# Projecting g by channels in two column tiles and turning it with four transposes, in an attention kernel on one core

## What is computed

```python
g     = (einsum('bchw,oc->bhwo', x, w_g) + b_g).reshape(B, N, Ci)
theta = (einsum('bchw,oc->bhwo', x, w_theta) + b_theta).reshape(B, N, Ci)
phi   = (einsum('bchw,oc->bohw', x, w_phi) + b_phi[:, None, None]).reshape(B, Ci, N)
att   = softmax(einsum('bnc,bcm->bnm', theta, phi), axis=-1)
y     = einsum('bnm,bmc->bnc', att, g).reshape(B, H, W, Ci)
out   = einsum('bhwc,oc->bohw', y, w_out) + b_out[:, None, None]
inv   = bn_gamma / sqrt(bn_var + 1e-5)
return x + out * inv[:, None, None] + (bn_beta - bn_mean * inv)[:, None, None]
```

## Time and profile before

| | |
|---|---|
| Runs | 204.07, 204.53, 207.46 us; median 204.53 us |
| Profiled execution | 204.88 us, its span 203.1 us |
| Mean granted clock of TensorE | 0.998 |
| PE busy | 193.6 us (95%) |
| PE weight loads busy | 133.3 us (66%) |
| DVE busy | 175.2 us (86%) |
| ACT busy | 136.2 us (67%) |
| POOL busy | 152.3 us (75%) |
| DMA moved | 35.28 MB, most packets under 512 B |

### The profile page before, as it was taken

The page is one execution under the profiler, slowest core; times in us unless marked ns, Lnnn a source line. Parts: engine busy times, 40 slices in busy tenths (PEclk is TensorE's granted clock), DMA queues, the critical chain, the costliest instruction groups (busy, mean ns, idle before and its releaser), DMA issues.

```text
span 203.1 us, 3988 instructions
## 1 busy us (share of the span) xinstructions
PE 193.6 (95%) x1100; PEld 133.3 (66%) x1100; DVE 175.2 (86%) x291; ACT 136.2 (67%) x245; POOL 152.3 (75%) x127
## 2 busy tenths in 40 slices
PE   7997889999999999999999999999999998999993
PEld 6575756686666857677666957677566956566551
DVE  0689898978997899978998899978998899989881
ACT  2866867768396856866587766866577675767731
POOL 2458898699779999699988999699988964954300
PEclk9999999999999999999999999999999999999999
DMA  6315998899999999899779997899998998847102
GB/s 156 97 34 163 225 114 174 185 221 175 186 227 232 217 163 231 184 257 207 187 163 253 229 215 168 161 246 189 195 214 181 223 170 181 138 76 155 52 3 103
DMA packets 59500, 35.28 MB, mean 174 GB/s; under 512 B 50400, under 2 KB 50912, under 8 KB 59488
## 3 DMA queue, kind: packets, MB, share of 16 engines
q1 hardware_dynamic: 59200, 35.01, 83.0%
q10 hardware_dynamic: 288, 0.14, 0.3%
HBM read 8.36 MB, written 4.23 MB: 62 GB/s over the span
## 4 chain that ended last, share of the span: by engine, by line
PE 70%; DVE 12%; DMA 5%; issue 4%; ACT 3%; SPq 1%; POOL 1%; ACTq 0%; POOLq 0%; DVEq 0%
PE ps_scores L743 22%; PE ps_flip L808 12%; PE ps_y L755 12%; PE ps_misc L769 6%; PE ps_y L762 6%; DVE neg_max L599 6%; PE ps_misc L727 5%; PE ps_misc L849 4%; DMA pt_hi<-p_hi 3%; DVE pt_lo L637 3%; DMA vec<-vectors_dram 2%; SPq L292 1%; DVE y_norm L616 1%; PE ps_scores L755 1%; ACT probs L532 1%
## 5 line engine op out<-in xcount | busy, mean ns | idle before, releaser
L532 ACT ACTIVATE probs<-ps_scores,neg_max 128x1024 f32<-128x1024 f32 x64 | 71.9, 1123 | 30.0 <-DVE neg_max L599 15.1
L599 DVE TENSOR_REDUCE neg_max<-ps_scores 128x1 f32<-128x1024 f32 x64 | 77.9, 1218 | 9.1 <-PE ps_scores L743 8.8
L637 DVE SCALAR_TENSOR_TENSOR pt_lo<-ps_flip,pt_hi 128x512 f16<-128x512 f32 x84 | 53.9, 684 | 5.4 <-ACT pt_hi L519 5.1
L519 ACT ACTIVATE pt_hi<-ps_flip 128x512 f16<-128x512 f32 x84 | 45.6, 595 | 14.2 <-PE ps_flip L808 14.2
L426 POOL TENSOR_TENSOR p_lo<-probs,p_hi 128x1024 f16<-128x1024 f32 x22 | 47.0, 2138 | 4.3 <-POOL p_hi L422 3.4
L743 PE MATMUL ps_scores<-phi_hh,theta_hl 128*128 128x512 f32 x128 | 47.1, 449 | 3.1 <-ACT probs L532 2.5
L808 PE MATMUL ps_flip<-ident,probs 128*128 128x128 f32 x336 | 44.5, 275 | 0.7 <-DVE pt_lo L637 0.7
L808 PEld LDWEIGHTS ps_flip<-ident,probs 128*128 128x128 f32 x336 | 38.1, 142 | 9.6 <-DVE pt_lo L637 2.5
L743 PE MATMUL ps_scores<-phi_ll,theta_hl 128*128 128x512 f32 x128 | 40.1, 394 | 0.0
L755 PE MATMUL ps_y<-pt_hi,g_parts 128*128 128x512 f16 x120 | 28.4, 379 | 0.5 <-issue 0.4
L422 POOL TENSOR_SCALAR p_hi<-probs 128x1024 f16<-128x1024 f32 x22 | 23.5, 1067 | 6.7 <-ACT probs L532 6.3
(11 more groups left out here) (79 smaller groups left out, 175.3 us busy)
## 6 DMA issues: line engine op xcount, KB each, us to landing
x_in<-x_in_dram SPq DMA_DIRECT2D x16, 256.0 KB, 3.3
inv_all<-inv_row SPq DMA_DIRECT2D x15, 256.0 KB, 4.0
out_dram<-resid SPq DMA_DIRECT2D x15, 256.0 KB, 2.8
phi_hh<-hi SPq DMA_DIRECT2D x14, 256.0 KB, 5.8
phi_ll<-lo SPq DMA_DIRECT2D x14, 256.0 KB, 6.1
theta_hl<-hi SPq DMA_DIRECT2D x7, 256.0 KB, 4.7
theta_hl<-lo SPq DMA_DIRECT2D x7, 256.0 KB, 5.6
pt_hi<-p_hi SPq DMA_TRANSPOSE x22, 4.0
```

The source lines that it names most:

```text
L519: nc.scalar.activation(pt_hi[ring][:, c * HALF_TILES:(c + 1) * HALF_TILES, slot * P:(slot + 1) * P], ps_flip[c][:, :].rearrange("p (a n) - ...
L532: nc.scalar.activation(probs[k % PROB_RING][:, :], ps_scores[k % 2][:, :], ACT.Exp, bias=neg_max[:, k % STEPS:k % STEPS + 1], accum_out=ro ...
L599: nc.vector.tensor_reduce(out=top, in_=ps_scores[k % 2][:, :], op=ALU.max, axis=AX.X, negate=True).then_inc(row_max_ready if by_dma(it, k) ...
L637: nc.vector.scalar_tensor_tensor(out=pt_lo[ring][where], in0=ps_flip[c][:, :].rearrange("p (a n) -> p a n", n=P), scalar=PROB_SCALE, in1=p ...
```

## The change

In image b at j = 4 nothing is projected any more. At j = 5, behind the low-half sum, PE projects g with the operands exchanged: `wg` (64 columns) is the stationary and 512 positions of `x_in` move, once into partitions 0 to 63 and once into 64 to 127 of `ps_misc`. The bank then holds channels on partitions and positions along the row. ACT evacuates this at j = 6 into the new tile `g_channels`; DVE takes the peak from there. At j = 7, where PE has no flips, it turns `g_channels` with four transposes into the second flip bank, ACT evacuates that bank into `g_raw` at its j = 7, and the flips at the next j = 0 wait for it before they write that bank. The convolution at j = 6 waits for the evacuation into `g_channels`, and POOL's split waits for the evacuated theta and phi instead of the projection of g.

```diff
--- before.py
+++ after.py
@@ -104,6 +104,7 @@
         phi_hh = [sbuf(f"phi_hh{i}", [P, N], F32R) for i in range(2)]
         phi_ll = [sbuf(f"phi_ll{i}", [P, N], F32R) for i in range(2)]
         g_raw = [sbuf(f"g_raw{i}", [P, MT, CI], F32) for i in range(2)]
+        g_channels = sbuf("g_channels", [P, BANK], F32)
         g_scaled = sbuf("g_scaled", [P, MT, CI], F32)
         g_parts = [sbuf(f"g_parts{i}", [P, MT, 2 * CI], F16) for i in range(2)]
         g_peak = sbuf("g_peak", [P, 2], F32)
@@ -165,6 +166,8 @@
         lo_ready = sem("lo_ready")
         g_ready = sem("g_ready")
         g_out = sem("g_out")
+        g_channels_out = sem("g_channels_out")
+        g_flipped = sem("g_flipped")
         g_peak_ready = sem("g_peak_ready")
         g_peak_spread = sem("g_peak_spread")
         g_peak_read = sem("g_peak_read")
@@ -440,7 +443,7 @@
                                             g_parts[r][:, :, 0:CI], ALU.subtract).then_inc(g_split, 1)
 
                 if j == 5 and exists(b + 2, B):
-                    hold(g_ready, b + 2)
+                    hold(proj_out, 2 * b + 2)
                     split_x(it * 16 + 16 * (k // STEPS + 2), r, 0)
                     split_x(b + 2, r, 1)
                 if j == 7 and exists(b + 2, B):
@@ -543,9 +546,15 @@
                     nc.scalar.activation(qk[:, c * BANK:(c + 1) * BANK], ps_misc[:, :], ACT.Identity,
                                          bias=BIAS_TP).then_inc(proj_out, 1)
 
-                if j == 5 and exists(image + 1, B):
+                if j == 6 and exists(image + 1, B):
                     act.wait_ge(g_ready, image + 2)
-                    evacuate_g(image + 1, ps_misc[:, :], g_raw[(k // MT + 1) % 2][:, :, :].rearrange("p t c -> p (t c)"))
+                    wait(act, g_peak_ready, image + 1)
+                    wait(act, g_flipped, image)
+                    nc.scalar.activation(g_channels[:, :], ps_misc[:, :], ACT.Copy).then_inc(g_channels_out, 1)
+                if j == 7 and exists(image + 1, B):
+                    act.wait_ge(g_flipped, image + 1)
+                    evacuate_g(image + 1, ps_flip[1][:, :].rearrange("p (a c i) -> p a c i", c=PER_IMAGE, i=CI),
+                               g_raw[(k // MT + 1) % 2][:, :, :].rearrange("p (c a) i -> p a c i", c=PER_IMAGE))
 
                 if j == 0:
                     exponential(it, k)
@@ -583,10 +592,15 @@
                                                op0=ALU.add, op1=ALU.subtract).then_inc(first_lo, 1)
 
             def peak_of_g(b, r):
-                dve.wait_ge(g_out, b + 1)
                 wait(dve, g_peak_spread, b - 1)
-                nc.vector.tensor_reduce(out=g_peak[:, r:r + 1], in_=g_raw[r][:, :, :], op=ALU.max, axis=AX.XY,
-                                        apply_absolute_value=True).then_inc(g_peak_ready, 1)
+                if is_first(b):
+                    dve.wait_ge(g_out, 1)
+                    nc.vector.tensor_reduce(out=g_peak[:, r:r + 1], in_=g_raw[r][:, :, :], op=ALU.max, axis=AX.XY,
+                                            apply_absolute_value=True).then_inc(g_peak_ready, 1)
+                else:
+                    dve.wait_ge(g_channels_out, b)
+                    nc.vector.tensor_reduce(out=g_peak[:, r:r + 1], in_=g_channels[:, :], op=ALU.max, axis=AX.X,
+                                            apply_absolute_value=True).then_inc(g_peak_ready, 1)
 
             def read_peak(b, r, spread):
                 dve.wait_ge(g_peak_spread, b + 1)
@@ -803,6 +817,8 @@
                         if isinstance(f, int) and f == 0:
                             pe.wait_ge(*((g_out, 1), (shift_ready, 1))[c])
                         wait(pe, pt_lo_ready, 2 * f + c - 1)
+                        if j == 0 and c == 1 and not in_last_half(t):
+                            wait(pe, g_out, image + 1)
                         for a in range(HALF_TILES):
                             m = c * HALF_TILES + a
                             last = nc.tensor.transpose(ps_flip[c][:, a * P:(a + 1) * P],
@@ -822,6 +838,14 @@
                     pe.wait_ge(g_split, image_at(it, k - 6) + 1)
                     wait(pe, y_scaled, h)
                     sum_high(ring, r, ps_y, slice(0, BANK), slice(0, BANK))
+
+                if j == 7 and exists(image + 1, B):
+                    pe.wait_ge(g_channels_out, image + 1)
+                    pe.wait_ge(pt_lo_ready, 2 * flip_at(it, k - 3) + 2)
+                    for a in range(HALF_TILES):
+                        last = nc.tensor.transpose(ps_flip[1][:, a * P:(a + 1) * P],
+                                                   g_channels[:, a * P:(a + 1) * P], ident[:, :])
+                    last.then_inc(g_flipped, 1)
 
                 t = tile_at(it, k + 1)
                 if exists(t, TILES):
@@ -852,15 +876,19 @@
                 h = half_at(it, k - 10)
                 if j % HALF_TILES == 2 and exists(h, HALVES - 2):
                     if more:
-                        pe.wait_ge(*((proj_out, 2 * image + 2) if j == 2 else (g_out, image + 2)))
+                        pe.wait_ge(*((proj_out, 2 * image + 2) if j == 2 else (g_channels_out, image + 1)))
                     else:
                         wait(pe, result_ready, h)
                     convolve(h, ps_misc[:, :], slice(0, BANK))
 
-                if j == 4 and more:
+                if j == 5 and more:
                     pe.wait_ge(proj_out, 2 * image + 2)
                     wait(pe, result_ready, 2 * image - 1)
-                    project_g(ps_misc, (k // MT + 1) % 2, range(MT)).then_inc(g_ready, 1)
+                    for c in range(PER_IMAGE):
+                        last = nc.tensor.matmul(ps_misc[c * CI:(c + 1) * CI, :], wg[:, :],
+                                                x_in[(k // MT + 1) % 2][:, c * BANK:(c + 1) * BANK],
+                                                start=True, stop=True, skip_group_check=True)
+                    last.then_inc(g_ready, 1)
 
 
                 if tile_is(it, k, 1):
```

## The result

The changed kernel takes 208.0 us (median of its runs) where the kernel before took 204.3 beside it: a ratio of 1.0137, 95% interval 1.0093 to 1.0182. It is slower, by less than 2%. The forecast was 207.4, a ratio of 1.014. The profiled execution took 208.06 us with a span of 206.2, 3.1 more than the earlier trace rows.

A forecast was written before the change was run, and what follows sets the result against it. The prediction took PE as the bound, its work laid nearly end to end; terms summed to +0.43 us an image, taken as +2.9 over seven images, giving 207.4 us from 204.53. Its range was 204.0 to 210.6.

The forecast's parts named there:

- Step 2: Tile 3's flips, now right behind tile 5's scores, wait for DVE's low part of tile 2: about +0.62 us an image.
- Step 3: Two column-tiled projections at j = 5 behind the low-half sum, overlapping only partly: +1.29 us an image, bounds 0.86 and 1.72.
- Step 1: The eight projections at j = 4 leave PE's chain: -1.73 us an image.
- step 4: Four PE transposes of g_channels added at j = 7: +0.44 us an image, bounds 0.4 and 0.6.
- the second rival: The two projections at j = 5 run wholly side by side, 0.86 us; image unchanged, 204.5 us; chance 0.16.
- Step 5: The convolution at j = 6 no longer waits for DVE's y_norm: -0.19 us an image, bounds -0.19 and 0.
- Step 6: One more ACT evacuation, and tile 7's exponential waiting at j = 7, stay hidden: 0 us, bounds 0 and +0.3.
- Step 7: DVE's peak, waiting for ACT's evacuation at j = 6, and POOL's x split with its changed hold: both 0.
- side by side: no change: Rival at j = 5: both projections overlap wholly, 0.86 us, image changes by 0.00; 204.5 us, chance 0.16.
- One after the other: Rival at j = 5: the column tiles run in single file, 1.72 instead of 1.29 us; 210.5 us, chance 0.25.
- The wait of step 2 does not show: Rival at tile 3's flips: no wait; 203.2 us with partial overlap (chance 0.05), 200.2 with whole overlap (0.04).

The follow-up runs named there:

- e6: Changed kernel with SP's DMA transpose of tile 1's high part issued ahead of the three low-part restacks; 205.7 us, ratio 1.0027.
- e1: Changed kernel with the two column-tiled projections back at j = 4 and their ACT evacuation at j = 5; 206.1 us, ratio 1.0034.
- e2p: Kernel before with its eight old projections moved to j = 5 and DVE's 128x2 scaling written as two 128x1 instructions; 209.2 us, ratio 1.0212.
- e4p: Changed kernel with g_raw's evacuation behind tile 7's exponential and DVE's 128x2 scaling written as two 128x1 instructions; 206.7 us, ratio 1.0057.
- e2: Kernel before with its eight old projections moved from j = 4 to j = 5, evacuation to j = 6; 218.85 us, ratio 1.0664.
- e4: Changed kernel with ACT's evacuation into g_raw moved behind tile 7's exponential; 213.9 us, ratio 1.0453.
- e3: Changed kernel with the pair of projections at full width, w_g padded with zero columns, accumulating one after the other; 212.8 us, ratio 1.0352.
- e8: Changed kernel with the pair at j = 4, tile 1's transpose ahead of low restacks, and 128x2 scaling as two 128x1; 203.2 us, ratio 0.9862.
- e10: Kernel before, old projections kept at j = 4, with tile 1's transpose ahead of low restacks and 128x2 scaling as two 128x1; 204.5 us, ratio 0.9976.
- e6b: Kernel before with SP's transpose of tile 1's high part issued ahead of the low-part restacks; 204.6 us, ratio 0.999.

## Why the prediction was right, and where it was not

The time was right, and by luck in good part: two terms were wrong, and the errors and the waits that had no term made up for each other. With steps 2 and 3 as measured the prediction's own sum is -1.73 + 0.83 + 0.86 + 0.44 - 0.19 = +0.21 an image, which would have given about 206 us. That is near what e6 takes, where PE no longer waits for tile 1's transfer: 205.7.

1. *Step 1* (-1.73) and *step 4* (+0.44): as measured.
2. *Step 2, what the projections covered* (+0.62, bounds to 0.7): the mechanism is right, shown by e1 (gone when covered) and by e2p (there when the old form is moved). The size was 0.83, above the upper bound; the step's own working gives 114.96 - 114.30 = 0.66, not 0.62. DVE's part was right to 0.01 (2.75 from the row maximum's start to the second half's end, as the earlier trace rows have it). What I left out is the restart: I ended the last four flips at half of 0.87, their distance in a running queue. After DVE's end at 115.54 + 1.29 = 116.83 the hand-over takes 0.05 (PE's weight loads start at 116.88) and the four flips 117.54 - 116.88 = 0.66 to their modelled end, together 0.71 where I had 0.54.
3. *Step 3, the pair* (+1.29): wrong. It takes 0.86; the second rival was right about it, and with it the rule that the prediction cites from the Trainium skill (TensorEngine Tiling (Array Packing), Key Properties). The queue order that I argued from does not hold the second side back. The 0.86 holds behind the low-half sum; behind work at full width the same pair takes 1.01 (e1).
4. *Step 5, the convolution* (-0.19): right at j = 6. But a wait of about the same size appears at j = 2 in some images, where I had nothing (the step to tile 4's scores is 3.68 instead of 3.52 in images 2 and 4).
5. *Step 6, ACT's gate*: it costs PE nothing by itself, as said, though the scores of the next tile 1 do wait (1.07 of the chain for 0.93) and those of tile 2 wait less. "Its transfer is wanted four steps on" looked at tile 7's own transfer only. The half microsecond by which POOL and SP run later goes on to the restacks and to tile 1's transfer behind them, and that was nearly late already: three waits, 1.9 us. e4p, in which POOL starts tile 7 earlier, has none of these waits in images 1 to 6.
6. *Step 7* ("both 0") did not look at POOL's instructions lying against DVE's. Here that cost the 0.4 us at j = 2 (518 ns a time instead of 235, held by POOL's high part); where POOL's low part lay there instead it cost 1.5 us an image (e2, and some images of e4).

The sum as measured, on the span: six images at +0.17 in the stretch that I had summed are 1.0; tile 1's transfer is 1.4 (2.3 us of it go with e6; about 0.9 of the same were there before, in the last steps of images 0 to 2); the convolution at j = 2 is about 0.4; the last 0.3 lies at the start and in image 7. That is 3.1. My forecast had 2.9 of PE work in one place; the trace has a third of it there.

Of the rivals, "side by side: no change" was right on the pair and wrong on the time, because step 2 was larger and because of the transfer. "One after the other" is excluded by the four records, which take 0.86 of the chain; the nearest thing to it that was built is the pair at full width (e3), 212.8. "The wait of step 2 does not show" is excluded by the chain.

## What to carry to other kernels

Before work is moved off a place on the bounding engine, ask what it covered there: this projection was PE work of 1.73 us that hid a wait of 0.83, and the cheaper form was worth something (0.15 an image, e8 against e10) only where it still hid it. Price a restart from standstill, not from a running queue. When two engines' order in time shifts by half a microsecond, look again at every transfer that was nearly late and at short instructions that may now meet a long one of the neighbour engine.

## What the runs showed of the hardware

- DVE's in-place scaling of 128x2 f32 in SBUF took up to 2.08 us when a POOL instruction of 2.14 us ran, and ended with it (within 0.04 us in e2); the same on 128x1 took 0.15 beside the same POOL work. In all, 13.3 us for seven instructions (e2) against 2.7 for the 22 single ones (e2p).
- Two f32 matmuls into the two column halves overlapped wholly, 0.86 for both behind other column-tiled work, though each leaves two records and the program gives one side first; 28 such records took 7.2 us, and 13.8 at full width (e3). The passage into column tiles cost 0.15 (1.01 instead of 0.86, e1), and the one back 0.15 (flips of 1.02 instead of 0.87).
- A transfer issued first was worth 2.3 us in one kernel (e6) and nothing that could be measured in its neighbour (e6b, ratio 0.9951 to 1.003).
